# Attention scores and their maxima in places of one PSUM bank instead of two, a quarter of the queries at a time

## What is computed

```
xn   = layernorm(x)
q, k, v = split(xn @ w_qkv)                 # 16 heads of 16
q, k = spectral_filter(q), spectral_filter(k)
attn = softmax(q @ k.T / 4) @ v             # 2048 x 2048 scores, 2 batches x 16 heads
h    = relu(xn @ W_fc.T) ** 2               # 256 -> 1024
y    = h @ W_proj.T                         # 1024 -> 256, then 5 spiking steps, averaged
out  = x + attn @ w_out + b_out + spikes(y)
```

## Time and profile before

| | |
|---|---|
| median of 3 runs | 1691.6 us (1691.25 to 1692.2) |
| span of the profiled execution | 1689.3 us |
| PE busy | 1681.4 us |
| DVE, ACT busy | 1494.2, 1330.1 us |
| chain that ended last | 98% PE |
| PE matmuls | 17842 |

### The profile page before, as it was taken

One profiled execution on the slowest core, in us unless ns is written; L12 is line 12 of the kernel. 1 busy time (PEld: TensorE's weight loads), 2 busy tenths in 40 slices (PEclk: granted clock), 3 DMA queues, 4 the chain that ended last, 5 costly groups with the idle time before them and its releaser, 6 DMA issues.

```text
span 1689.3 us, 44435 instructions
## 1 busy us (share of the span) xinstructions
PE 1681.4 (100%) x17842; PEld 1145.9 (68%) x17842; DVE 1494.2 (88%) x2375; ACT 1330.1 (79%) x1718; POOL 719.7 (43%) x979
## 2 busy tenths in 40 slices
PE   9999999999999999999999999999999999999999
PEld 6566666666666666666666666666666666666667
DVE  6889999998999999989998999999989998999884
ACT  5548888888888888888888888888888888888872
POOL 3103334555433345554333455543335554333455
PEclk9999999999999999999999999999999999999999
DMA  6851122112211221122112211221122112211133
GB/s 216 294 161 47 33 54 55 51 33 55 55 50 34 55 55 43 41 55 55 43 41 55 56 37 47 55 55 36 48 55 56 31 53 55 55 30 54 43 105 103
DMA packets 95406, 108.02 MB, mean 64 GB/s; under 512 B 56032, under 2 KB 70240, under 8 KB 95200
## 3 DMA queue, kind: packets, MB, share of 16 engines
q1 hardware_dynamic: 91744, 101.97, 21.2%
q10 hardware_dynamic: 3456, 3.21, 0.6%
HBM read 78.91 MB, written 20.97 MB: 59 GB/s over the span
## 4 chain that ended last, share of the span: by engine, by line
PE 98%; DVE 1%; ACT 0%; issue 0%; ACTq 0%; POOL 0%; POOLq 0%
PE banks L735 31%; PE ring L711 22%; PE ring L718 14%; PE ring L724 14%; PE banks L841 7%; PE banks L846 3%; PE banks L659 2%; PE ring L928 2%; PE ring L672 1%; PE ring L645 1%; PE ring L659 1%; PE ring L686 0%; DVE stats L947 0%; DVE attnT L979 0%; ACT xnT L513 0%
## 5 line engine op out<-in xcount | busy, mean ns | idle before, releaser
L562 ACT ACTIVATE probs<-ring 128x1024 f32<-128x1024 f32 x1024 | 1002.1, 1026 | 6.5 <-PE ring L724 6.2
L711 PE MATMUL ring<-kst,qst 64*128 64x512 f32 x2000 | 674.7, 417 | 0.3 <-ACT probs L562 0.3
L735 PE MATMUL banks<-probs,vst 128*32 128x256 f32 x8192 | 548.2, 385 | 0.1
L1036 DVE TENSOR_REDUCE pmax<-ring 128x2 f32<-128x1024 f32 x407 | 497.7, 1223 | 12.7 <-PE ring L711 0.5
L568 ACT ACTIVATE half_sb<-ring 128x512 f32<-128x512 f32 x500 | 299.2, 598 | 261.4 <-PE ring L711 254.1
L718 PE MATMUL ring<-qst,kst 64*128 64x512 f32 x2048 | 493.0, 425 | 0.1
L711 PEld LDWEIGHTS ring<-kst,qst 64*128 64x128 f32 x2000 | 328.3, 184 | 208.3 <-issue 204.6
L1017 DVE TENSOR_REDUCE pmax<-ring 128x1 f32<-128x512 f32 x500 | 345.4, 691 | 88.7 <-PE ring L711 85.1
L724 PE MATMUL ring<-shift_rows,ones 64*128 64x512 f32 x2048 | 422.9, 390 | 0.0
L1023 DVE TENSOR_REDUCE pmax<-half_sb 128x1 f32<-128x512 f32 x500 | 335.5, 671 | 37.0 <-ACT half_sb L568 33.1
L735 PEld LDWEIGHTS banks<-probs,vst 128*32 128x32 f32 x8192 | 213.7, 109 | 209.7 <-issue 91.0
(11 more groups left out here) (96 smaller groups left out, 1050.9 us busy)
## 6 DMA issues: line engine op xcount, KB each, us to landing
kst<-qk_scratch SPq DMA_DIRECT2D x256, 128.0 KB, 3.0
qst<-qk_scratch SPq DMA_DIRECT2D x256, 128.0 KB, 2.9
qk_scratch<-attnT SPq DMA_DIRECT2D x32, 256.0 KB, 3.0
shift_rows<-shiftT SPq DMA_DIRECT2D x512, 2.0 KB
qk_scratch<-probs SPq DMA_DIRECT2D x16, 256.0 KB, 3.0
attnT<-o_turned SPq DMA_DIRECT2D x256, 16.0 KB, 1.9
xnT<-x SPq DMA_DIRECT2D x8, 512.0 KB, 5.6
out<-xnT SPq DMA_DIRECT2D x7, 512.0 KB, 2.9
```

Of the source, the lines that this page charges most:

```text
L562: act.activation(probs[:, s % PS, :], score_slot(g), ACT.Exp, scale=SCALE).then_inc(exp_done, 1)
L711: return pe.matmul(unit_slot(g)[:, c * BLK:(c + 1) * BLK], qst[b][rows, tile * P:(tile + 1) * P], kst[b][rows, key:key + BLK], start=True, ...
L735: mm = pe.matmul(po[32 * j:32 * (j + 1), half * D:(half + 1) * D], vst[b][:, kt, :], quarters[:, j], start=(kt == 0), stop=(kt == TB - 1))
L1036: dve.tensor_reduce(pmax[:, tile, 2 * part:2 * part + 2], unit_slot(g).rearrange("p (c e) -> p c e", c=2), AX, ALU.max).then_inc(mx_taken, 1)
```

## The change

A tile of scores becomes one bank: 128 keys against 512 queries. A unit then has 64 of these (`MINI`), in four quarters of queries with 16 tiles each, and works them in quads of four (`opening_quad` at the head of a quarter, `later_quad` three times). ACT takes exponentials of 512 columns, and PE's `times_v` has 128 columns in each matmul, 32 matmul instructions behind each quad. Every maximum is one bank too and is reduced from PSUM by one DVE instruction; the copy by ACT is gone. Scores have three banks and maxima three. A tile's score matmul is followed at once by its shift on the same half of the array; with each quad one half (`far`) has the four maxima and two of the tiles, the other (`near`) the feed-forward share and two tiles.

```diff
+CHAINS = 3
+PLACES = 3
+SCORE_BANKS = (1, 4, 5)
+MAX_BANKS = (0, 2, 3)
-PS = 4
+PS = 8
...
-        probs = sb("probs", [P, PS, HALF])
+        probs = sb("probs", [P, PS, BLK])
...
-            def take_half(p):
-
-                act.wait_ge(half_ready, p + 1)
-                act.wait_ge(half_max, p)
-                act.activation(half_sb[:], unit_slot(2 * p)[:, BLK:2 * BLK], ACT.Copy).then_inc(half_taken, 1)
...
-                act.activation(probs[:, s % PS, :], score_slot(g), ACT.Exp, scale=SCALE).then_inc(exp_done, 1)
+                act.activation(probs[:, g % PS, :], score_bank(g), ACT.Exp, scale=SCALE).then_inc(exp_done, 1)
...
+            def maximum(x, side):
...
+                pe.wait_ge(mx_taken, n + 3 - PLACES)
+                pe.matmul(max_bank(x), qst[b][rows, tile * P:(tile + 1) * P], kst[b][rows, chunk * BLK:(chunk + 1) * BLK],
+                          start=True, stop=True).then_inc(mx_ready, 1)
+
+            def bank_free(g):
+
+                if g in (1, 2):
+                    pe.wait_ge(v_taken, NB + 1)
+                if g >= CHAINS:
+                    pe.wait_ge(exp_done, g + 1 - CHAINS)
+
+            def first_score(g, side):
...
+                bank_free(g)
+                pe.matmul(score_bank(g), kst[b][rows, kt * P:(kt + 1) * P], qst[b][rows, q:q + BLK],
+                          start=True, stop=False)
+                pe.matmul(score_bank(g), ones[rows, :], shift_rows[rows, q:q + BLK],
+                          start=False, stop=True).then_inc(score_ready, 1)
+
+            def times_v(first, last):
+
+                pe.wait_ge(exp_done, last + 1)
+                for g in range(first, last + 1):
...
+                    quarters = probs[:, g % PS, :].rearrange("p (t j q) -> p j t q", j=4, q=32)
+                    for j in range(4):
+                        mm = pe.matmul(po[32 * j:32 * (j + 1), quarter * P:(quarter + 1) * P], vst[u % 2][:, kt, :],
+                                       quarters[:, j], start=(kt == 0), stop=(kt == TB - 1))
+                    mm.then_inc(pv_done, 1)
...
+            def opening_quad(u, quarter):
+
+                g, near, far = MINI * u + TB * quarter, 1, 0
+                maximum(g, far)
+                first_score(g, near)
+                first_score(g + 1, far)
+                share(u, quarter, 0, 0)
+                share(u, quarter, 0, 1)
+                maximum(g + 1, far)
+                share(u, quarter, 0, 2)
+                maximum(g + 2, far)
+                share(u, quarter, 0, 3)
+                maximum(g + 3, far)
+                first_score(g + 2, near)
+                first_score(g + 3, far)
+                if g:
+                    times_v(g - QUAD, g - 1)
+
+            def later_quad(u, quarter, n):
+
+                g, near = MINI * u + TB * quarter + QUAD * n, 1 - n // 2
+                far = 1 - near
+                maximum(g, far)
+                first_score(g, near)
+                share(u, quarter, n, 0)
+                first_score(g + 1, far)
+                maximum(g + 1, far)
+                share(u, quarter, n, 1)
+                share(u, quarter, n, 2)
+                maximum(g + 2, far)
+                first_score(g + 2, far)
+                share(u, quarter, n, 3)
+                first_score(g + 3, near)
+                maximum(g + 3, far)
+                times_v(g - QUAD, g - 1)
...
+            def next_max(x):
+                n = FIRST_MAX + x
+                tile, chunk = chunk_of(n % CHUNKS)
+                dve.wait_ge(mx_ready, n + 1)
+                dve.tensor_reduce(pmax[:, tile, chunk:chunk + 1], max_bank(x), AX, ALU.max).then_inc(mx_taken, 1)
...
-                if s == LEAD + 2:
+                if m == LEAD - 1:
                     for link in range(4):
-                        split_shift(link, 2 * i + 1, 1, FIRST_MAX + g - 2)
+                        split_shift(link, 2 * i + 1, 1, CHUNKS * (i + 1))
```

## The result

The changed kernel takes **1773.3 us** (median, 1772.6 to 1774.6) against 1691.9 (1691.3 to 1692.6) for the kernel before on the same chip: ratio **1.0482** (1.0467 to 1.0497). The forecast was 1755 with a range of 1725 to 1812; the sign and the range held, the size fell 18 us short. The profiled execution has a span of 1772.3 us, 83.0 more than before.

What follows compares the result with a forecast made beforehand. PE was taken as the only limit; 54.6 us for 31 units, 0.3 and 7.9 for the last unit and 0.4 at the start made 63 us on 1689.3, with 2.3 for the median 1755 us, range 1725 to 1812.

Steps and rivals of the forecast that it cites:

- What bounds the kernel: Whole kernel: PE alone is the limit, so lighter ACT and DVE work is worth nothing; slower by over 0.2% given 0.88.
- The halves run apart: PE's array: a half is not held by matmuls queued on the other, so the eighth place still starts at 1.71 us.
- Strict order: Rival: PE starts matmuls strictly in program order; later quads 3.50 us, opening ones 3.27, total 1926 us; 5%.
- The bank of the first tile is wanted for the fourth: Later quads: the fourth tile's load waits for the first tile's exponential, until 1.41 us; quad 3.07 us instead of 3.04.
- The sign that I had named for this wait: Sign of being right: short waits of PE's loads for the exponentials (L560's line) in every quad.
- `times_v` +0.02: `times_v`: eight waves of 128 columns instead of four of 256 add 0.02 us a quad, bounds 0 and 0.07.
- The fourth maximum of an opening quad waits for the first: Opening quads: PE's fourth maximum waits for DVE until 1.28 us, delaying the last score on that half; quad 3.17 us.
- `split_shift` moves to just before an opening quad: Twice a unit: DVE's small steps delay the fourth maximum by a further 0.35 us; those opening quads take 3.52 us.
- The first quad: Start of the kernel: four more `up` matmuls of 0.11 us, +0.4 us in all.
- The last unit: Last unit: first quarter +0.3 us; then quads stay at 3.07 where pairs took 2.56 and 2.13, +7.9 us.
- the one with harder waits: Rival inside the range: exponential takes 0.65 us, two hops 0.03 longer each; later quads grow 0.11, total 1800 us.
- The one with shrinking places: Rival, faster: a place on the halves costs 0.21 us, not 0.23; some 1630 us, about 1670 with half; 8%.

Runs made afterwards that it cites:

- the experiment with the kernel before: Each 256-column `times_v` matmul made into two of 128 columns, against the kernel before, nothing else changed: 1697.3 us, ratio 1.0033.

## Why the prediction was right, and where it was short

- **What bounds the kernel, and that the order would turn a free change into a slower one**: right. ACT lost 127 us of work and PE gained by none of it.
- **The halves run apart.** Right in the new order too: of the two L710 from 990.16 the second is the far half's; its record of 0.39 ends 0.72 behind the first's start, so it starts at 990.49, while the near half's share (L732), which stands before it in the program, starts at 990.73. Strict order, by the prediction's sum, would have made a quad of 3.50.
- **The bank of the first tile is wanted for the fourth**: right in each of its steps (0.77, 0.595, 1.42 against 0.76, 0.60, 1.41). Halving the exponential takes 0.034 off a quad, once DVE and POOL are out of the way. But the later quad is 3.088 and not 3.07: in the rows above the last shift starts at 1.76 where the sum has 1.74, and `times_v` 0.33 behind it where the sum has 0.31. The 0.018 between 3.07 and 3.088, by 12 by 31, are 7 us. The sign that I had named for this wait, short waits of PE's loads for the exponentials in every quad, did not show: the page has 5.7 us of them in the whole kernel. (I also gave a wrong line for the exponential, L560 for L546.)
- **`times_v` +0.02**: the sum's value was too high by 0.010, as the experiment with the kernel before shows.
- **The fourth maximum of an opening quad waits for the first**: 3.18 against 3.17, and both ways of removing it (another order, shorter maxima) take it to 3.09. The step's mechanism is shown.
- **`split_shift` moves to just before an opening quad** is the step whose size failed. The sum has 0.35 of further delay. With POOL out of the way it is 0.26 and 0.29 (3.44 and 3.47 over 3.18): the small steps take 0.76 until the next reduction starts (993.32 to 994.08) where I took 0.81, and the rest of the difference was not traced. The 0.81 was the mean of 0.75 and 0.86, the alternate lengths in the kernel before, and I did not ask why they alternate. The longer ones have the cast of 0.28 beside POOL's L466, so the kernel before already showed that POOL can lengthen DVE's small steps. The prediction prices waits for POOL at nothing; PE waits for POOL nowhere in its own waits, but what POOL costs DVE reaches PE. Moved to new places, the cast met POOL's first instruction of the recurrence in 31 of 31 units and was 0.62 instead of 0.17. That is 0.38 above the 3.52 in the second place and 0.08 under it in the first: 0.30 by 31, or 9 us, to which the quads of 4.31 add 1.7. That the two misses had opposite signs was luck.
- **The first quad** of all was costed with its four `up` matmuls alone, +0.4. The first `times_v` starts at 121.24 where it was 118.22, 3.0 later, so 2.6 us are missing in the sum. Two things are in them for which I had no term. PE stands idle from 114.36 to 115.84, where the chain of work runs through an exponential (0.59) and ACT's `relu_sb` (0.50). Then PE's granted clock falls to half, its level of 1.2 GHz, from 117.52 to 120.94. The chain of work before and inside that stretch (start us, us, what), and the stretches themselves (PEclk is the number ahead of the last two):

```profile
117.23 0.23 PE ring L712 x2
...
120.65 0.42 PE ring L712 x2
```

```profile
114.40:117.50 3.10, 1.66 (x17) 1.35 (x18) 1.12 (x3) 1.39 (x4) 1.38 (x2) 1.00 0.91 234
117.60:120.90 3.30, 3.30 (x20) 2.97 (x18) 2.55 (x5) 2.11 (x4) 0.00 (x0) 0.50 0.66 179
121.00:125.00 4.00, 4.00 (x78) 3.11 (x80) 3.03 (x6) 3.00 (x6) 0.00 (x0) 1.00 0.02 4
```

  A place of 512 columns costs 0.42 there and not 0.23. Half of the 3.4 us, 1.7, is my estimate of the loss. The profiled runs with POOL later and with DVE's steps at other places have the same stretch and start their first `times_v` at 121.35 and 121.32. Those with another order of the opening quad and with half the maxima have PE idle for as long (1.49 and 1.48 us), keep the full clock and start it at 119.87 and 119.81. What decides it is not shown.
- **The last unit** took +7.7 where the sum has +7.9 and +0.3.

Together: units (50.79 - 50.22) x 31 = 17.7, the start 2.6, the last unit -0.5: 19.8 us, which is the span's 83.0 less the 63.2 of the sum.

Of the rivals, the one with harder waits has the right sign for what is left. The one with shrinking places needed the bank back within 0.56 us of the shift's end; it came back after 0.69 (990.89 to 991.58). Where the readers were halved it came back sooner, and a quad was still 3.02 to 3.08 and no less: the place does not shrink to 0.21.

## What to carry to other kernels

When tiles shrink, count how often each bank goes round between two points where its engine rests; a wait that was met a step earlier comes to stand inside the step and is paid in every one. A matmul that waits for another engine should stand behind the matmuls of its half that can run, which was worth 0.09 us in an opening quad here. And small steps of DVE on a path that PE waits for should be kept apart in time from POOL's instructions, since an edit that moves either by 0.02 us can change them from 0.17 to 0.62 or 1.05 us. Where the same steps alternate between two lengths, as 0.75 and 0.86 did in the kernel before, look at what stands beside the longer ones before taking the mean.

## What the runs showed of the hardware

- The engine that the profile names as a releaser may have held nothing: 410 waits of 0.36 us under ACT's name went to "issue" when ACT got faster, at the same length.
- Two engines' instructions that start within about 0.01 us of each other fall one way in most units and the other in some: L964 at 0.17 in nearly all units and 1.05 in two of the changed kernel, nine with another order of PE. A mean over units hides it; single quads of 4.31 among quads of 3.44 gave it away.
- An edit that makes one engine faster can bring such a meeting about. Exponentials of 0.38 us instead of 0.595 made the first split quad 0.69 us longer, in every unit, and the second 0.40 shorter.
- Not every meeting costs as much: a cast of 0.17 us that met a `tensor_tensor` of POOL ended with it (0.62 us), and one that met a `tensor_scalar` of 0.86 us took 0.28 and ended 0.44 before it.
- A slice of the page can hide a change of PE's clock: 3.4 us at half the clock stand in a slice of 44 us that still reads 9.
- On column strips, eight waves of 128 columns took 0.010 us more than four of 256.
- Taking out every second `times_v` as a pause lost more than the switch saved: with `times_v` behind every second quad, 97.7 us more than behind every one (1827.3 against 1729.6).
